# A graph network on one core: GpSimd takes some one-hots and column sums, small loads move to another queue, TensorE gets idle-time matmuls

## The reference, cut to what matters

```
_L0: three times  x = relu(D^-1/2 (A + I) D^-1/2 (x W) + b)          # A from src, dst, edge_weight
_L1: attention over the edges of each target, four heads
_L2: z = concat(x[dst], x[src], edge_attr); gate = sigmoid(z @ W_f + b_f); core = softplus(z @ W_s + b_s)
     return x + segment_sum(gate * core, dst)
_L3: ten times  out = gelu(layernorm(A_norm (out W) + b)), and an identity branch
x = layernorm(x + _L0(x)); x = layernorm(x + _L1(x)); x = layernorm(x + _L2(x)); x = layernorm(x + _L3(x))
```

## Time and profile before

| | us |
|---|---|
| median of 3 runs | 3285.01 (3284.21 to 3285.78) |
| the profiled execution | 3285.47 |
| its span | 3283.5 |
| TensorE busy | 3106.7 (95%) |
| DVE busy | 1370.8 (42%) |
| ScalarE busy | 1408.2 (43%) |
| GpSimd busy | 846.8 (26%) |
| adjacency units, first to last product | 35.4 to 224.8 |
| gate steps | 1308 to 1840 |
| ten layers of _L3 | 1842 to the end |

### The profile page before, as it was taken

How to read it: one execution, slowest core, us unless ns; L and a number is a source line. 1 busy time by engine, 2 the same in 40 slices (tenths; PEclk the granted TensorE clock), 3 DMA queues, 4 the chain that set the end, 5 groups by cost and what they waited for, 6 DMA issues and landing times. The chain is left out here.

```text
span 3283.5 us, 45208 instructions
## 1 busy us (share of the span) xinstructions
PE 3106.7 (95%) x14568; PEld 2006.1 (61%) x14568; DVE 1370.8 (42%) x3096; ACT 1408.2 (43%) x2506; POOL 846.8 (26%) x939
## 2 busy tenths in 40 slices
PE   7879999979999998999999799999999999999998
PEld 6865555547788775777777555555555555555554
DVE  7971110125666667999999511111111111111112
ACT  6860000225555555888888423333332222222333
POOL 2010000037777763777777000000000000000000
PEclk8989999989999998999999899999999999999999
DMA  2556667723333323666666467666677766777774
GB/s 90 231 236 243 273 282 286 286 61 83 87 83 83 83 70 92 186 194 184 186 185 183 181 288 288 283 284 281 284 287 290 290 281 281 290 291 298 290 298 169
DMA packets 166699, 709.29 MB, mean 216 GB/s; under 512 B 39287, under 2 KB 133090, under 8 KB 153423
## 3 DMA queue, kind: packets, MB, share of 16 engines
q1 hardware_dynamic: 127865, 618.84, 48.5%
q0 software_dynamic: 33600, 83.09, 9.1%
q10 hardware_dynamic: 5011, 4.48, 0.5%
HBM read 657.91 MB, written 48.07 MB: 215 GB/s over the span
## 5 line engine op out<-in xcount | busy, mean ns | idle before, releaser
L1422 PE MATMUL deep_out_psum<-deep_adjacency,deep_scaled_nodes_odd 125*128 125x450 f32 (+1 forms) x1750 | 669.7, 537 | 0.0
L1422 PE MATMUL deep_out_psum<-deep_adjacency,deep_scaled_nodes 125*128 125x450 f32 (+1 forms) x1750 | 669.7, 537 | 0.0
L1670 POOL DMA_INDIRECT source_rows<-gat_source_rows,pair_src x416 | 396.5, 953 | 575.3 <-POOLq L64 448.8
L1422 PEld LDWEIGHTS deep_out_psum<-deep_adjacency,deep_scaled_nodes_odd 125*128 125x128 f32 x1750 | 328.4, 189 | 299.8 <-issue 298.9
L1422 PEld LDWEIGHTS deep_out_psum<-deep_adjacency,deep_scaled_nodes 125*128 125x128 f32 x1750 | 328.1, 189 | 298.9 <-issue 298.0
L2100 POOL DMA_INDIRECT near_room<-gate_source_rows,pair_src x416 | 395.1, 950 | 141.7 <-issue 119.2
L1480 ACT ACTIVATE deep_squares_high<-deep_aggregate,deep_vectors 128x450 fp32r<-128x450 f32 (+1 forms) x70 | 46.7, 668 | 618.1 <-DVE deep_aggregate L1552 618.1
L1422 PE MATMUL gcn_out_psum<-adjacency_columns,gcn_scaled_nodes 125*128 125x450 f32 (+1 forms) x700 | 268.7, 538 | 0.0
L2198 PE MATMUL gate_banks<-edge_weights,edge_features_t 128*128 128x256 f32 x832 | 248.4, 380 | 0.0
L1566 DVE SCALAR_TENSOR_TENSOR deep_normed<-deep_aggregate,deep_vectors,deep_squares 128x450 f32<-128x450 f32 (+1 forms) x70 | 47.9, 684 | 384.9 <-ACT deep_squares L1489 384.9
L1422 PEld LDWEIGHTS gcn_out_psum<-adjacency_columns,gcn_scaled_nodes 125*128 125x128 f32 x700 | 131.2, 190 | 123.5 <-issue 122.8
(11 more groups left out here) (418 smaller groups left out, 4754.0 us busy)
## 6 DMA issues: line engine op xcount, KB each, us to landing
deep_adjacency<-adjacency SPq DMA_DIRECT2D x69, 5625.0 KB, 16.2
adjacency_columns<-adjacency SPq DMA_DIRECT2D x19, 5625.0 KB, 16.1
adjacency<-adjacency_columns SPq DMA_DIRECT2D x7, 5625.0 KB, 17.7
edge_features<-in_edge_attr_dram SPq DMA_DIRECT2D x416, 64.0 KB
att_node_rows<-pair_dst_rows SPq DMA_DIRECT2D x104, 128.0 KB
gate_node_rows<-pair_dst_rows SPq DMA_DIRECT2D x104, 128.0 KB, 3.3
source_rows<-gat_source_rows,pair_src POOLq DMA_INDIRECT x416, 2.5
near_room<-gate_source_rows,pair_src POOLq DMA_INDIRECT x416
```

Source lines behind the costliest of these rows:

```text
L1422: m = nc.tensor.matmul(op[:, n % 2, 0:cols], h[l % 2][:, s, :], ring[0:T, n % 2, s, 0:cols], start=s == 0, stop=s == NS - 1)
L1670: pool.indirect_dma_start(xj[:, b % HOLD, q, :], None, d["h_r"], bass.IndirectOffsetOnAxis(ap=c["pair_src"][:, b * PQ + q:b * PQ + q + 1], ...
```

## The change

In the adjacency stage, three things. First, GpSimd makes `ohr` for units with n % 3 = 0 and j of 9 or more (`bypool`; in block 0 only up to n = 21), with three one-column comparisons each in place of DVE's one instruction for the unit; TensorE waits for them with one more semaphore (`s_po`). These are 36 of 174 units. Second, GpSimd makes the extra blocks' tables one block ahead: those of block 0 before all loops, and in the loop pass for extra block i those of block i + 1. Third, the loads of the extra blocks leave SyncE's list and are issued by ScalarE: the first behind unit 21, each further one in ScalarE's loop behind its copy of the product before.

In the gate stage GpSimd makes six of the seven folds, behind its gathers; DVE makes the last only. The stage's block ends without GpSimd's drain. TensorE gets 30 matmuls of 512 columns whose product nobody reads (`keep_busy`): 16 before the last but one scatter, 8 before the last, 6 behind it.

```
@@ -374,6 +374,7 @@
         EARLY = 4
+        POOL_FROM = EXTRA_AT + RING + 2
         tab = c["lane_words"]
...
         cell = c["h_t"][:, 0:RING * SUB * CELLS].rearrange("p (k q i) -> p k q i", k=RING, q=SUB)
@@ -400,20 +401,21 @@
         byact = [n for n in range(len(units)) if n % 3 == 1]
+        bypool = [n for n, (b, j, u) in enumerate(units) if n % 3 == 0 and j >= POOL_FROM and (b > 0 or n < LISTED_AT + 3)]
...
                 eng.wait_ge(s_xl, 1)
-            return [eng.value_load(c["extra_bounds"][0:1, b + k:b + k + 1], min_val=k, max_val=UO) for k in range(2)]
+            return [eng.value_load(c["extra_bounds"][0:1, b + k:b + k + 1], min_val=k, max_val=UO - 1) for k in range(2)]
...
         def _(pool):
@@ -427,13 +429,27 @@
             for b in range(NSP):
+                for n in (n for n in bypool if units[n][0] == b):
+                    u, k = units[n][2], n % RING
+                    g0, m = u[0], len(u)
+                    if n >= RING:
+                        pool.wait_ge(s_mm, n - RING + 1)
+                    for q in range(m):
+                        i = g.tensor_scalar(ohr[:, k, q, 0:T], c["ramp"][:, 0:T], tab[:, 0, g0 + q:g0 + q + 1], None, ALU.is_equal)
+                    i.then_inc(s_po, 1)
+                if b == 0:
+                    pool.wait_ge(s_om, 32)
+                    g.tensor_tensor(local[:, :], more[:, 1:2], first_cell[:, :], ALU.subtract).then_inc(s_loc, 1)
+                    g.tensor_scalar(xohr[:, 0:T], c["ramp"][:, 0:T], more[:, 0:1], None, ALU.is_equal)
+                    pool.wait_ge(s_loc, 1)
+                    g.tensor_scalar(xcell[:, :], c["ramp"][:, 0:CELLS], local[:, 0:1], more[:, 2:3], ALU.is_equal, ALU.mult).then_inc(s_oo, 1)
                 lo, hi = bounds(pool, b)
                 with pool.Fori(lo, hi) as i:
-                    wait_alone(pool, c, s_om, (i + 1) * 32)
-                    wait_alone(pool, c, s_omm, i + 1)
+                    wait_alone(pool, c, s_om, (i + 2) * 32)
+                    wait_alone(pool, c, s_omm, i + 2)
                     g.tensor_tensor(local[:, :], more[:, 1:2], first_cell[:, :], ALU.subtract).then_inc(s_loc, 1)
                     g.tensor_scalar(xohr[:, 0:T], c["ramp"][:, 0:T], more[:, 0:1], None, ALU.is_equal)
-                    wait_alone(pool, c, s_loc, i + 1)
+                    wait_alone(pool, c, s_loc, i + 2)
                     g.tensor_scalar(xcell[:, :], c["ramp"][:, 0:CELLS], local[:, 0:1], more[:, 2:3], ALU.is_equal, ALU.mult).then_inc(s_oo, 1)
@@ -491,7 +507,7 @@
                     marks_of(h + 1)
-                if n not in byact:
+                if n not in byact and n not in bypool:
                     vec.tensor_tensor(ohr[:, k, 0:m, 0:T], c["ramp"][:, 0:T].unsqueeze(1).to_broadcast([128, m, T]),
...
                 dve.wait_ge(s_mk, h + 1)
@@ -549,6 +565,8 @@
                     pe.wait_ge(s_ao, byact.index(n) + 1)
+                if n in bypool:
+                    pe.wait_ge(s_po, bypool.index(n) + 1)
                 if n >= BANKS:
...
                 for q in range(len(u)):
@@ -596,6 +614,10 @@
                     nc.scalar.copy(xsum[:, :], xacc[:, 0:CELLS]).then_inc(s_oc, 1)
+                    e0 = act.value_load(c["extra_first"][0:1, bass.ds(i + 1, 1)], min_val=0, max_val=E)
+                    act.dma_start(more[0:EL, :], d["edges"][bass.ds(e0, EL), :]).then_inc(s_om, 16)
+                    act.dma_start(first_cell[:, :], c["extra_cells"][:, bass.ds(i + 1, 1)]).then_inc(s_om, 16)
+                return hi
...
                 if n in byact:
@@ -610,9 +632,16 @@
                     onehots(n + EARLY)
+                if n == LISTED_AT:
+                    act.wait_ge(s_p, 2)
+                    act.wait_ge(s_xl, 1)
+                    e0 = act.value_load(c["extra_first"][0:1, 0:1], min_val=0, max_val=E)
+                    act.dma_start(more[0:EL, :], d["edges"][bass.ds(e0, EL), :]).then_inc(s_om, 16)
+                    act.dma_start(first_cell[:, :], c["extra_cells"][:, 0:1]).then_inc(s_om, 16)
                 if b >= 1 and j == EXTRA_AT:
                     extras(b - 1)
-            extras(NSP - 1)
+            extra = extras(NSP - 1)
+            wait_alone(act, c, s_om, (extra + 1) * 32)
             act.wait_ge(s_in, 1)
@@ -624,12 +653,6 @@
             for b in range(NSP):
-                lo, hi = bounds(sp, b)
-                with sp.Fori(lo, hi) as i:
-                    e0 = sp.value_load(c["extra_first"][0:1, bass.ds(i, 1)], min_val=0, max_val=E)
-                    wait_alone(sp, c, s_oo, i + 1)
-                    sp.dma_start(more[0:EL, :], d["edges"][bass.ds(e0, EL), :]).then_inc(s_om, 16)
-                    sp.dma_start(first_cell[:, :], c["extra_cells"][:, bass.ds(i, 1)]).then_inc(s_om, 16)
                 sp.wait_ge(s_blk, b + 1)
...
                 sp.dma_start(c["degree_parts"][0:NS, first:first + BW], stage[T:T + 1, slot[b], :, :]).then_inc(s_dg, 16)
@@ -2070,13 +2093,13 @@
-        block = ctx.enter_context(nc.Block())
+        block = ctx.enter_context(nc.Block(no_gpsimd_drain=True))
@@ -2101,6 +2124,11 @@
                 pool.wait_ge(s_g[b % 4], 16 * PQ * (b // 4 + 1))
+            for j in range(NSP - 1):
+                c0, n = SPANS[j]
+                pool.wait_ge(s_O, PQ * (DONE[j] + 1))
+                nc.gpsimd.tensor_tensor(c["h_t"][:, c0:c0 + n], c["h_t"][:, c0:c0 + n], odd[:, c0:c0 + n], ALU.add).then_inc(s_fp, 1)
+            pool.wait_ge(s_fp, NSP - 1)
@@ -2200,6 +2228,11 @@
                 m.then_inc(s_z, 1)
+
+            def keep_busy(n):
+                pe.wait_ge(s_et, NPB)
+                for _ in range(n):
+                    nc.tensor.matmul(p_e[:, :], rows[:, 0, 0, 0:128], rows[:, 0, 1:3, :].rearrange("r s f -> r (s f)"), start=True, stop=True)
...
                 pe.wait_ge(s_msg, b + 1)
@@ -2231,9 +2264,13 @@
                     core(b + 1)
+                else:
+                    keep_busy(16)
                 if b >= 1:
                     scatter(b - 1)
+            keep_busy(8)
             scatter(NPB - 1)
+            keep_busy(6)
@@ -2398,13 +2435,11 @@
-            def fold(b):
-                for j, (c0, n) in enumerate(SPANS):
-                    if DONE[j] == b:
-                        dve.wait_ge(s_O, PQ * (b + 1))
-                        cols = slice(c0, c0 + n)
-                        vec.tensor_tensor(c["h_t"][:, cols], c["h_t"][:, cols], odd[:, cols], ALU.add).then_inc(s_fin, 1)
-                        dve.wait_ge(s_fin, j + 1)
+            def fold_last():
+                c0, n = SPANS[NSP - 1]
+                dve.wait_ge(s_O, PQ * (DONE[NSP - 1] + 1))
+                vec.tensor_tensor(c["h_t"][:, c0:c0 + n], c["h_t"][:, c0:c0 + n], odd[:, c0:c0 + n], ALU.add).then_inc(s_fin, 1)
+                dve.wait_ge(s_fin, 1)
...
             for i in range(NG_ + 3):
@@ -2448,14 +2483,11 @@
                     merge(b - 1)
-                if 1 <= b < NPB - 1:
-                    fold(b - 1)
                 if b % 3 == 0 and b + 3 < NPB:
...
             message(NPB - 1)
-            fold(NPB - 2)
             merge(NPB - 1)
-            fold(NPB - 1)
+            fold_last()
```

8 lines of the change are left out of this document (4 added, 4 removed).

## The result

The changed kernel is slower, by 0.6%: 3304.85 us (median of 4 executions, 3303.08 to 3305.85) beside 3285.40 for the kernel before (4 executions, 3284.21 to 3286.71), a ratio of 1.0059 (95% interval 1.0047 to 1.0071). The profiled execution took 3304.27 us. The forecast was 3276.8 with a range up to 3286.0, so it is wrong in sign and the time lies outside the range.

What follows compares the result with a forecast made beforehand. DVE was taken to bound the adjacency stage, ScalarE close behind. Adjacency 3.4, gate 4.1 and next stage's head 0.65 us sum to 8.2 off 3285.47, so 3277.3, as median 3276.8 us; range 3269.5 to 3286.

Steps and rivals of the forecast that it cites:

- Which engine bounds the stage: Adjacency windows: DVE bounds, busy 24.2 of 25 us, with ScalarE close behind at 22.1.
- 7.0 less 2.0: Adjacency: 7.0 us won by moving one-hots to GpSimd, 2.0 lost where a block's first comparisons come late.
- The price of a comparison: Adjacency: three GpSimd comparisons take 2.3 us a unit, one in three slowed by contention; this fits.
- The load's price: Adjacency, extra blocks: 1.94 us from the second load's issue on ScalarE to GpSimd's start.
- the fourth rival: A load on ScalarE's queue is stuck behind a store: up to 17.5 us lost, 3294 us; chance 0.04.
- Late comparisons: Adjacency: GpSimd's first comparisons in a block wait behind the extra-table loop, 8.8 us in all; 2.0 us lost.
- ScalarE's sum of 121.5 us: Adjacency, 124 units: ScalarE's units 112.0, extra-block loops 4.0, loads 5.5 us; a gain of 8.6 at best.
- the 14 us to be won: Adjacency: upper bound of the one-hot gain, from 26 DVE one-hots at 0.55 us each.
- ScalarE takes it all back: Rival: ScalarE's loads and waits cost what DVE gives; 3.2 us won, 3281.9 us; chance 0.17.
- The double block: Adjacency, block 5 with two extra blocks: products 7.0 us apart instead of 4.46; 2.6 us lost.
- The gate: End of the gate stage: folds 1.9 and 1.3, scatter at full clock 0.9; 4.1 us won.
- The head: First products of the next stage: 0.65 us won, the middle between nothing and 1.3 if the clock holds.

Runs made afterwards that it cites:

- units_only: Kernel before plus only GpSimd's comparisons for 36 units, loads still on SyncE, old gate: 3724.14 us on a slow-gather chip, ratio 1.0053 to the kernel before.
- units_gate: Kernel before plus GpSimd's comparisons for 36 units and the new gate end, loads and tables as before: 3272.44 us, ratio 0.9962 to the kernel before.
- store_waits: Changed kernel with SyncE issuing a block's store only when the extra block's load has landed: 3713.37 us on a slow-gather chip, ratio 1.002 to the kernel before.
- spare_issues: sync_loads with ScalarE also issuing the changed kernel's two loads per extra block into tables nobody reads: 3750.89 us, one execution, slow-gather chip.
- sync_loads: Changed kernel with the extra blocks' loads issued by SyncE again, tables still one block ahead: 3268.48 us, ratio 0.9952 to the kernel before.
- gate_no_fill: Kernel before plus the new gate end without its 30 fill products, adjacency unchanged: 3281.67 us, ratio 0.999 to the kernel before.
- adj_only: Kernel before plus the adjacency part of the change alone: 3732.32 us on a slow-gather chip, ratio 1.0062 to the kernel before.
- no_pool_units: Changed kernel without the units' comparisons on GpSimd; loads stay on ScalarE and tables one ahead: 3284.11 us, one execution.

## Why the prediction was wrong

What VectorE, GpSimd and the gate would give was forecast well. The price of moving the loads to ScalarE was not, in two steps, and they turned the gain into a loss.

- **Which engine bounds the stage.** Right: with its one-hots taken away VectorE gives time up, A 192.5 to 184.9 and 186.0. I had 7.0 less 2.0; 5.7 is what units_only has over the mean of the three unchanged ones (191.7). Over the five blocks for which the 7.0 was worked out, the sums lie 122.9 (units_gate) and 122.6 us (units_only) apart in place of 129.7, so 6.8 and 7.1. That ScalarE alone is then the bound isn't shown: from 85 to 110 us of units_gate it is busy 23.8 of 25, and VectorE 24.2, as before.
- **The price of a comparison.** Right: half took at most 0.604 us in the changed kernel and the longest 1.307. In the 60 to 262 us window their mean is 0.643, so 1.93 for a unit; I had said 2.3. The Trainium skill's rule (GPSIMD Engine Reference, Key points) would have given 2.8. The trace agrees that there is contention, but less: 19 of 107 comparisons took over 0.70 us and one over 1.05.
- **The load's price: the step that failed.** I took 1.94 from issue to GpSimd's start for every load, from the earlier trace rows, a place with no store under way. Only the fourth rival asked about stores, and only whether an *earlier* one was still running. What happens is that SyncE's *own* store of that block waits for the same sum and goes out 0.4 to 1.3 us behind the load. Two loads then took 5.01 and 11.23. Of the 8.8 us way in "Late comparisons", 1.94 became 11.2 in the last block, and TensorE stood 8.72. store_waits prices it: some 12 us. The trace of the kernel before had a warning, the 13 us of the loads issued behind a store. The sum in that part is also off: 1.5 + 2 x 0.4 is 2.3, not 2.0.
- **ScalarE's issues: the second step that failed.** I priced a pair at 1.1, laid it in ScalarE's sum of 121.5 us over five blocks and let it come out of the 14 us to be won. The traces have 1.75 a pair, and the place decides more than the sum: the pair stands between two copies that free TensorE's banks, all five of which are full, so TensorE waits up to 2.30. spare_issues prices the issues at 17.7 over the stage, of which 13.6 lie in the five blocks for which the sum had 5.5. The rival "ScalarE takes it all back" had the right engine; it had capped the loss at the gain.
- **The first block was left out.** The first load now stands behind ScalarE's copy of a unit, and its second issue comes at 67.55, not 64.16; the first sum is 2.7 late (75.43 beside 72.73), 0.55 of it because the first product is. It isn't the load that costs: in spare_issues, whose useful loads are SyncE's, the first sum comes 39.0 after the first product (36.5 in sync_loads, 39.5 in the changed kernel), so it is ScalarE's issuing once more. I had named no term for it.
- **The double block.** Right: 7.0 apart for the products was forecast, 7.13 measured (206.94 to 214.07). The sums lie 6.45 apart, 3.01 before, 3.4 lost (2.6 forecast, though 7.0 - 4.46 is 2.5). With the loads on SyncE this loss is gone (2.3 apart), so it too belongs to the queue.
- **The gate.** 4.9 won where 4.1 were forecast, the scatter's 1.16 and hidden folds as said. By gate_no_fill the folds are worth 4.0 (3.2 forecast) and the fills 1.7 to 2.0 (0.9 forecast). Sixteen fills took 3.62 (3.4 forecast). GpSimd's fold took 1.14 (1.13 forecast). The missing drain bought nothing: from the last fold to SyncE's first issue it is 1.8 us (1856.29 to 1858.11), 1.7 before.
- **The head.** Wrong in sign: 2.9 lost, not 0.65 won. I had bounded it by 0 and 1.3, as if the clock could at worst fall as late as before; it fell at the barrier and stayed low over the whole head. Two pairs at 1.87 - 1.02 are 1.7, not 1.3, and that much can be had: store_waits, where the clock never falls there, has a head 1.6 shorter than before. Which of these a kernel gets is not explained by its code near there.

Step by step through the kernels, by means of those that share an adjacency: unchanged 191.7; comparisons on GpSimd 185.5, so -6.2; cells one ahead on SyncE's queue 180.8, so -4.7; ScalarE issuing for nothing 197.9, so +17.1; ScalarE's loads in use but never late 200.9, so +3.1 (the double block, whose sums lie 6.4 apart and not 2.6); the changed kernel 213.0, so +12.1 for the late loads. adj_only, the same adjacency with one load later still, has 218.8. The steps aren't independent: on ScalarE's queue GpSimd's comparisons *cost* 15.6 (197.4 to 213.0), on SyncE's they save 8.4 (188.6 to 180.2). The net of the first two is 10.9 won, more than my 3.4 for the whole stage; the move of the loads turned it into 21 lost.

## What to carry to other kernels

Before a small load is moved to another queue, look at what its new queue's engine does right behind it and who is full by then: 1.75 us of issuing between two copies that free banks cost 1.3 to 4 us a block here, while on SyncE it cost nothing that shows. Look also at the large transfer that the same event releases, and at what stands behind the engine that waits for the load: a load that took 9.8 us was free where its waiter had nothing else to do (no_pool_units) and cost 6.4 us of TensorE where comparisons were queued behind it (adj_only). Two good edits (comparisons on GpSimd, tables one ahead) were hidden by the third; taken without it, and with the gate's new end, they make the kernel 0.5% faster than before.
